# A fused attention and mixture-of-experts kernel: gathers set ahead of scatter-adds one tile behind, the shared weights fetched behind the last context rows, the first scores ahead of the second bias fold

## The chip, the cores and the metric

One Trainium2 chip, one of its cores. The metric is the device time of one execution in microseconds, the median of several runs. Before the change: 547.0 us, three runs from 546.81 to 549.09.

## The reference

`x` is 16 sequences of 56 rows of 512; each has a context of 1500 rows of 512. In float32:

```python
xn = layernorm(x)
Q  = xn @ Wq + bq;  K = ctx @ Wk + bk
x  = x + softmax(Q @ K.T / sqrt(512)) @ ctx         # 16 sequences, 56 x 1500 scores each
hn = layernorm(x)                                   # 896 rows
s  = sigmoid(hn @ gate.T) + bias                    # 16 experts
w, idx = top_k(s, 4);  w = w / (sum(w) + 1e-20)     # 4 experts of each row
out = sum over picked experts e of  w_e * (silu(hn @ Wg_e.T) * (hn @ Wu_e.T)) @ Wd_e.T
out = out + (silu(hn @ Sg.T) * (hn @ Su.T)) @ Sd.T  # a shared expert, for all rows
x   = x + out
```

The experts' inner width is 256. Which rows go to which expert is known only when the gate has run.

## The kernel before

**Attention.** The two projections are folded into one matrix, Wq Wk^T (`fold`), and two bias terms: a column for the queries' side (`fold_cols`) and a row (`fold_c`, `c_row`). Sequences go in 8 pairs, two side by side in the 128 lanes. A pair's context comes twice: transposed in four blocks (`ctx_cols`, 1.5 MB each) for the scores and as rows in three groups (`ctx_rows`, 2 MB each) for the weighted sum. There is one set of each, so SP reloads a block as soon as TensorE has used it (`cols_used`, `rows_used`). SP's queue works its transfers off in order; behind the first pair's rows it issues the shared expert's weights (`shared_raw`) and a block of zero rows, and only then the second pair's blocks. While a pair is scored, the gate and the rank of each row in its experts' lists are worked out for the pair before it.

**Shared stage.** 7 tiles of 128 rows go through the shared expert (t = 0 to 6). ScalarE casts its weights to a high part and VectorE takes the rest to a low part, so that each product is three fast matmuls (hi*hi, hi*lo, lo*hi). Meanwhile VectorE makes the plan: tables of 48 entries, one entry for each expert tile (which list column, which expert, which weights to split before it, how many turns). `lay_tables` puts them into one row, and each engine reads its entries by `value_load` (an instruction TENSOR_LOAD on its queue). The lists of rows (`list_at` to gather from, `list_to` to add to) have one column for each expert and tile.

**Expert stage.** 34 tiles of gathered rows here (t = 7 to 40), in the order of the experts, 11 turns of weights. Two buffers of each kind; tile t uses buffer t % 2. TensorE's order in one step t is: transpose z(t-1), the low part of up(t), transpose the gathered tile t+1, down(t-1), the high part of up(t+1). ScalarE in its step t: zt_hi(t-1), tanh(t), taken_hi(t+1), `keep_y(t-2)` (copies down's result to `y_sb`, once the scatter-add that read this buffer has landed), `name_add(t-2)` (copies the row numbers of that add), and the casts of weights that the plan asks for. VectorE: zt_lo(t-1), silu(t), taken_lo(t+1), the weight of each row of tile t+1, `name_take(t+3)` (the row numbers of a gather), and the low parts of the weights.

POOL issues all gathers and scatter-adds, in order, and waits in between:

```python
add(t, 1 - k)          # waits: adds of earlier experts landed, add_named, ysb_ready of t
gather(t + 5, k)       # waits: take_named of t + 5
```

An add reads and writes rows of `out` in HBM. Adds of one expert never meet in a row; an add waits until all adds of earlier experts have landed. SP loads a turn's weights (`w_raw`, 1.5 MB) when the low parts of two turns before are done, and waits for their landing.

## Time and profile before

| | |
|---|---|
| median of 3 runs | 547.0 us |
| the profiled execution | 546.24 us |
| its span | 544.5 us |
| mean granted TensorE clock | 0.96 |
| one turn of the attention loop on TensorE | 29.43 us (scores start at 66.11, 95.54, 124.97) |
| last third of attend, first shared matmul | 274.02 to 277.6, 277.61 us |
| gathered tile 13's taken_hi | 364.05 us |
| ScalarE casts of expert weights, L897 | 33, mean 1047 ns |
| VectorE low parts of them, L1280 | 33, mean 1223 ns |
| last scatter-add issued | 532.9 us |

Times of an execution are a little more than its span, which runs from the first to the last instruction of the trace. All start times in the text count from the span's start. Lines (L459) are lines of the kernel before. TensorE's clock has two levels here, 1.2 and 2.4 GHz; the granted clock is a share of 2.4. `L680` is the helper of all expert matmuls, `L500` all transposes of four blocks. A gather is `taken<-h_rows,take_at`, a scatter-add `out<-y_sb,add_at`.

### The profile page before, as it was taken

What the parts mean: (1) busy time and instruction counts of PE and PEld (TensorE: products, weight loads), DVE (VectorE), ACT (ScalarE), POOL (GpSimd) and SP (SyncE); (2) the same over time, 40 slices, a digit from 0 to 9 for tenths busy, and PEclk for the clock granted to TensorE, in tenths of its full rate; (3) what the DMA queues carried; (4) which work ended last, traced back from release to release, by engine and by line L of the source; (5) the groups of instructions that cost most, each with busy time, mean ns of one, the idle gap of its engine ahead of it and who ended that gap; (6) DMA issues with size and microseconds to landing.
All of it is one profiled execution on the core that took longest, in us unless ns stands there. A gap on an engine that the chain in (4) does not pass through costs nothing.

```text
span 544.5 us, 10804 instructions
## 1 busy us (share of the span) xinstructions
PE 481.4 (88%) x2472; PEld 291.5 (54%) x2473; DVE 260.0 (48%) x707; ACT 155.8 (29%) x303; POOL 119.3 (22%) x100
## 2 busy tenths in 40 slices
PE   4999999999999999998789869779998898899960
PEld 1565354453636363543358636567776666676740
DVE  3223345462737354352537864625565466555420
ACT  0001321020202020210213253435455456444430
POOL 1000000000000000000002233335554465335531
PEclk9989999999999999999899979979999899899985
DMA  9999999999999999999646676785858687445452
GB/s 212 393 419 427 398 424 415 409 427 396 424 402 426 403 422 404 422 426 415 258 127 174 150 202 191 235 254 94 221 100 265 137 207 210 78 88 98 98 64 32
DMA packets 28231, 149.04 MB, mean 274 GB/s; under 512 B 4072, under 2 KB 4200, under 8 KB 16424
## 3 DMA queue, kind: packets, MB, share of 16 engines
q1 hardware_dynamic: 15832, 123.08, 57.1%
q0 software_dynamic: 8720, 20.21, 20.5%
q10 hardware_dynamic: 3664, 5.57, 3.3%
q8 instruction: 7, 0.11, 0.1%
q14 instruction: 8, 0.07, 0.0%
HBM read 133.84 MB, written 15.01 MB: 273 GB/s over the span
## 4 chain that ended last, share of the span: by engine, by line
PE 49%; DMA 33%; issue 7%; DVE 3%; ACT 2%; POOLq 1%; ACTq 1%; POOL 1%; DVEq 1%; SPq 0%
DMA ctx_cols<-in_ctx_t 15%; PE b L680 13%; PE scores L550 11%; PE b L574 8%; DMA taken<-h_rows,take_at 8%; DMA out<-y_sb,add_at 5%; PE b L538 4%; PE b L500 4%; PE scores L512 2%; PE scores L680 2%; PE b L564 1%; DMA w_qk<-in_wk 1%; DMA out<-y_sb,shared_at 1%; DMA h_rows<-h 1%; POOL out L459 1%
## 5 line engine op out<-in xcount | busy, mean ns | idle before, releaser
L550 PE MATMUL scores<-ctx_cols,g_t 128*64 128x500 f32 x384 | 85.2, 586 | 2.6 <-DMA ctx_cols<-in_ctx_t 2.5
L574 PE MATMUL b<-ctx_rows,probs_t 125*64 125x512 f32 (+1 forms) x384 | 86.0, 598 | 0.0
L459 POOL DMA_INDIRECT out<-y_sb,add_at x34 | 54.5, 1604 | 89.0 <-ACT add_at L931 46.8
L423 POOL TENSOR_TENSOR rstd<-var_eps,neg_half 128x1 f32<-128x1 f32 x16 | 8.8, 549 | 268.4 <-DVE var_eps L1022 268.4
L680 PE MATMUL b<-w_hi,taken_hi 128*128 x136 | 56.2, 414 | 1.1 <-ACT taken_hi L908 1.1
L680 PE MATMUL b<-w_lo,taken_hi 128*128 x136 | 54.8, 403 | 0.0
L1280 DVE TENSOR_TENSOR w_lo<-w_raw,w_hi (+1 forms) x33 | 39.7, 1223 | 30.2 <-ACT w_hi L897 26.6
L550 PEld LDWEIGHTS scores<-ctx_cols,g_t 128*64 128x64 f32 x384 | 26.1, 136 | 51.8 <-issue 46.0
L574 PEld LDWEIGHTS b<-ctx_rows,probs_t 125*64 125x64 f32 (+1 forms) x384 | 26.3, 137 | 48.0 <-issue 47.1
L444 POOL DMA_INDIRECT taken<-h_rows,take_at x34 | 42.7, 1257 | 28.4 <-DVE take_at L1306 20.2
L897 ACT CAST w_hi<-w_raw (+1 forms) x33 | 33.8, 1047 | 29.0 <-PE b L680 9.1
L500 PE MATMUL b<-cst,taken 128*128 128x128 f32 x164 | 26.6, 287 | 17.1 <-DMA taken<-h_rows,take_at 15.2
L680 PE MATMUL b<-w_hi,taken_lo 128*128 x136 | 40.0, 416 | 0.0
L1053 DVE TENSOR_REDUCE row_max<-scores 128x1 f32<-128x1500 f32 x8 | 13.8, 1721 | 50.4 <-PE scores L550 50.4
L836 ACT COPY h_t_now<-b 128x512 f32<-128x512 f32 x7 | 4.1, 585 | 110.6 <-PE b L500 110.6
L500 PEld LDWEIGHTS b<-cst,taken 128*128 128x128 f32 x164 | 19.5, 146 | 28.3 <-issue 25.8
L1299 DVE TENSOR_TENSOR taken_lo<-b,taken_hi 128x512 fp32r<-128x512 f32 x41 | 28.1, 685 | 11.6 <-ACT taken_hi L908 11.6
L538 PE MATMUL b<-xn_t,w_fold 128*128 128x128 f32 x256 | 32.0, 286 | 1.4 <-ACT xn_t L820 1.4
L680 PEld LDWEIGHTS b<-w_hi,taken_hi 128*128 128x128 f32 x136 | 26.8, 197 | 11.0 <-issue 4.9
L908 ACT CAST taken_hi<-b 128x512 fp32r<-128x512 f32 x41 | 24.0, 587 | 30.1 <-PE b L500 28.6
L538 PEld LDWEIGHTS b<-xn_t,w_fold 128*128 128x128 f32 x256 | 30.7, 200 | 1.9 <-issue 1.0
L918 ACT CAST zt_hi<-b 128x256 fp32r<-128x256 f32 x41 | 15.2, 371 | 54.4 <-PE b L703 54.1
(213 smaller groups left out, 677.2 us busy)
## 6 DMA issues: line engine op xcount, KB each, us to landing
ctx_rows<-in_ctx SPq DMA_DIRECT2D x48, 1024.0 KB, 19.5
ctx_cols<-in_ctx_t SPq DMA_DIRECT2D x32, 1500.0 KB, 22.8
w_raw<-in_experts SPq DMA_DIRECT2D x11, 1536.0 KB, 7.5
h_rows<-h ACTq DMA_DIRECT2D x16, 115.5 KB
taken<-h_rows SPq DMA_DIRECT2D x7, 264.0 KB, 3.1
out<-xs ACTq DMA_DIRECT2D x2, 784.0 KB
shared_raw<-in_shared SPq DMA_DIRECT2D x1, 1536.0 KB, 32.4
xs<-in_x ACTq DMA_DIRECT2D x12, 112.0 KB
```

Of the source, the lines that this page charges most:

```text
L444: nc.gpsimd.indirect_dma_start(taken[i][:, :], None, h_rows[:, :], bass.IndirectOffsetOnAxis(ap=take_at[i][:, 0:1], axis=0)).then_inc(gath ...
L459: nc.gpsimd.indirect_dma_start(out[:, :], bass.IndirectOffsetOnAxis(ap=add_at[i][:, 0:1], axis=0), y_sb[:, i * DIM:(i + 1) * DIM], None, c ...
L500: last = nc.tensor.transpose(bank[:, k * P:(k + 1) * P], src[:, k * P:(k + 1) * P], ident)
L538: last = nc.tensor.matmul(b7[:, m * P:(m + 1) * P], w_fold[:, k, m * P:(m + 1) * P], xn_t[:, k, :], start=(k == 0), stop=(k == KD - 1))
L550: last = nc.tensor.matmul(scores[HALF * b:HALF * (b + 1), n, 0:CHUNK], g_t[:, k, HALF * b:HALF * (b + 1)], ctx_cols[:, at:at + CHUNK], sta ...
L574: last = nc.tensor.matmul(b3[HALF * b:HALF * (b + 1), :], probs_t[0:rows_in(p), at:at + HALF], ctx_rows[0:rows_in(p), g, b, c * DIM:(c + 1 ...
L680: return nc.tensor.matmul(bank, a[:, k, :], w[:, bass.ds(at + k * n, n)], start=start, stop=stop)
L897: nc.scalar.copy(w_hi[:, bass.ds(at, THIRD)], w_raw[:, bass.ds(at, THIRD)]).then_inc(hi_ready, 1)
L908: nc.scalar.copy(taken_hi[:].rearrange("p k n -> p (k n)"), b4[:, :]).then_inc(taken_hi_ready, 1)
L918: nc.scalar.copy(zt_hi_cols[:], b5[:, 0:INNER]).then_inc(zt_hi_ready, 1)
L1280: nc.vector.tensor_tensor(w_lo[:, bass.ds(at, THIRD)], w_raw[:, bass.ds(at, THIRD)], w_hi[:, bass.ds(at, THIRD)], ALU.subtract).then_inc(l ...
L1299: nc.vector.tensor_tensor(taken_lo[:].rearrange("p k n -> p (k n)"), b4[:, :], taken_hi[:].rearrange("p k n -> p (k n)"), ALU.subtract).th ...
```

## The change

1. SP issues `shared_raw` and the zero rows behind the last pair's context rows. ScalarE's three casts and VectorE's three low parts move from behind the first pair to behind the last pair's probabilities.
2. The query bias column is no longer made by 40 narrow matmuls, but by four wide ones into b4, whose diagonal blocks VectorE sums out. The scalar bq*bk comes from VectorE and one matmul. The first two score blocks stand ahead of `fold_c`.
3. The row numbers of the tiles are picked once: the list of places is transposed on TensorE (`lay_places`), kept by ScalarE and multiplied by a 0/1 matrix (`pick_tiles`), so that tile t has its own column in `tile_at` and `tile_to`. Reads of the plan for them fall away on VectorE and ScalarE.
4. A gather is issued ahead of the scatter-add, for the tile six ahead, and waits for the transposes of the tile that had its buffer. The add's row numbers are copied by POOL. On VectorE the weight and the name of the next gather stand ahead of silu.
5. SP issues the loads of the first two turns' weights one behind the other.

```diff
@@ SP
-            sp.dma_start(shared_raw[:], shared).then_inc(shared_loaded, 16)
-            sp.wait_ge(init_ready, 1)
-            sp.dma_start(h_rows[TOKENS:TOKENS + P, :], zero_rows[:]).then_inc(init_stored, 16)
...
             reload_cols(PAIRS - 2)
             reload_rows(PAIRS - 2)
+            sp.dma_start(shared_raw[:], shared).then_inc(shared_loaded, 16)
+            sp.wait_ge(init_ready, 1)
+            sp.dma_start(h_rows[TOKENS:TOKENS + P, :], zero_rows[:]).then_inc(init_stored, 16)
...
             load_raw(0)
             load_raw(1)
+            sp.wait_ge(raw_first, 16)
+            sp.sem_inc(raw_ready, THIRDS)
+            raw_there(1)
@@ POOL
             def gather(t, i):
                 pool.wait_ge(take_named, t - (SHARED - 1))
                 settle(pool)
+                pool.wait_ge(tt_ready, t - 1)
+                settle(pool)
...
             def add(t, i):
                 first = entry(pool, T_FIRST, t - SHARED, TILES + SHARED)
-                pool.wait_ge(added[0], pool.snap((first + 1) // 2 * 16 + 16, min_val=16, max_val=16 * TILES))
+                pool.wait_ge(added[i], t // 2 * 16 + 16)
                 settle(pool)
-                pool.wait_ge(added[1], pool.snap(first // 2 * 16 + 16, min_val=16, max_val=16 * TILES))
-                settle(pool)
-                pool.wait_ge(add_named, t - (SHARED - 2))
+                nc.gpsimd.tensor_copy(add_at[i][:], tile_to[:, bass.ds(t - SHARED, 1)]).then_inc(add_named, 1)
+                others = first // 2 if i == 0 else (first + 1) // 2
+                pool.wait_ge(added[1 - i], pool.snap(others * 16 + 16, min_val=16, max_val=16 * TILES))
                 settle(pool)
                 pool.wait_ge(ysb_ready, t + 1)
+                settle(pool)
+                pool.wait_ge(add_named, t + 1)
...
-            add_shared(3)
             pool.wait_ge(init_stored, 16)
             pool.wait_ge(h_stored, PAIRS * 32 + 16)
...
             gather(SHARED, 1)
             gather(SHARED + 1, 0)
+            add_shared(3)
             add_shared(4)
             gather(SHARED + 2, 1)
             gather(SHARED + 3, 0)
             add_shared(5)
             gather(SHARED + 4, 1)
             add_shared(6)
+            gather(SHARED + 5, 0)
...
                     t = pair * 2 + (SHARED + k)
+                    gather(t + 6, 1 - k)
                     add(t, 1 - k)
-                    gather(t + 5, k)
@@ TensorE
-                for m in range(KD):
-                    for k in range(KD):
-                        last = nc.tensor.matmul(b7[:, m:m + 1], wk_sb[:, k, m * P:(m + 1) * P], bq_sb[:, k:k + 1],
-                                                start=(k == 0), stop=(k == KD - 1))
                 for k in range(KD):
-                    last = nc.tensor.matmul(b7[:, KD:KD + 1], bq_sb[:, k:k + 1].to_broadcast([P, P]),
-                                            bk_sb[:, k:k + 1], start=(k == 0), stop=(k == KD - 1))
+                    last = nc.tensor.matmul(b4[:, :], bq_sb[:, k:k + 1].to_broadcast([P, P]), wk_sb[:, k, :],
+                                            start=(k == 0), stop=(k == KD - 1))
...
+            def lay_places():
+                pe.wait_ge(plan_ready, 1)
+                pe.wait_ge(places_ready, 1)
+                nc.tensor.transpose(scores[:, 2, 0:P], place_at[:], ident).then_inc(places_laid, 1)
+            def pick_tiles():
+                pe.wait_ge(places_kept, 1)
+                nc.tensor.matmul(scores[:, 2, P:P + AHEAD], place_t[:], tile_picks[:], start=True, stop=True
+                                 ).then_inc(tiles_picked, 1)
...
             project(0)
+            score(0, 0)
+            score(0, 1)
             fold_c()
-            for k in range(KD):
-                score(0, k)
+            score(0, 2)
+            score(0, 3)
...
             shared_transpose(6)
+            lay_places()
             down(4, 0, shared_hi, shared_lo, 0)
+            pick_tiles()
@@ ScalarE
-            act.wait_ge(shared_loaded, 16)
-            act.wait_ge(fold_ready, KD + 2)
-            for n in range(THIRDS):
-                nc.scalar.copy(shared_hi[:, n * THIRD:(n + 1) * THIRD], shared_raw[:, n * THIRD:(n + 1) * THIRD]
-                               ).then_inc(shared_hi_ready, 1)
...
             store_h(last_pair - 1)
+            act.wait_ge(shared_loaded, 16)
+            act.wait_ge(fold_ready, KD + 3)
+            for n in range(THIRDS):
+                nc.scalar.copy(shared_hi[:, n * THIRD:(n + 1) * THIRD], shared_raw[:, n * THIRD:(n + 1) * THIRD]
+                               ).then_inc(shared_hi_ready, 1)
...
                 keep_y(t - 2, i)
-                if not isinstance(t, int):
-                    name_add(t - 2, i)
                 more_thirds(t + 1)
@@ VectorE
             def name_take(t, i):
-                col = entry(dve, T_COL, t - SHARED, LISTS + EXPERTS - 1)
-                nc.vector.tensor_copy(take_at[i][:], list_at[:, bass.ds(col, 1)]).then_inc(take_named, 1)
+                nc.vector.tensor_copy(take_at[i][:], tile_at[:, bass.ds(t - SHARED, 1)]).then_inc(take_named, 1)
             def take_weight(t, i):
-                e = entry(dve, T_EXPERT, t - SHARED, EXPERTS - 1)
-                nc.vector.tensor_copy(taken_w[:, i:i + 1], taken[i][:, bass.ds(e + DIM, 1)]).then_inc(w_ready, 1)
+                dve.wait_ge(gathered[i], (t - SHARED) // 2 * 16 + 16)
...
+                nc.vector.scalar_tensor_tensor(picked_w[:, i * EXPERTS:(i + 1) * EXPERTS], iota16, expert_row[:, bass.ds(t - SHARED, 1)],
+                                               taken[i][:, DIM:ROW], ALU.is_equal, ALU.mult, accum_out=taken_w[:, i:i + 1]
+                                               ).then_inc(w_ready, 1)
...
             def step(t, i):
                 z_to_lo(t - 1)
+                take_weight(t + 1, 1 - i)
+                name_take(t + 3, 1 - i)
                 silu_rows(t, i)
                 taken_to_lo(t + 1)
-                take_weight(t + 1, 1 - i)
-                name_take(t + 3, 1 - i)
                 more_thirds(t + 1)
```

One step of POOL's loop in the expert stage, before (L459 is the add, L444 the gather, 1024x512 the whole of `out`):

```order
L323 TENSOR_LOAD plan
L323 ISA x2
L451 ISA
L453 ISA
L455 REGISTER_ALU
L457 REGISTER_ALU
L459 DMA out<-y_sb,add_at 1024x512
L442 REGISTER_ALU
L444 DMA taken<-h_rows,take_at 128x528
```

and after (L469 is the gather, L486 the add):

```order
L467 REGISTER_ALU
L469 DMA taken<-h_rows,take_at 128x528
L335 ISA
L335 TENSOR_LOAD plan
L335 ISA x2
L476 ISA
L478 ISA
L478 COPY add_at<-tile_to 128x1
L480 ISA
L482 REGISTER_ALU
L486 DMA out<-y_sb,add_at 1024x512
```

The gather now stands first, and between it and the add there is one more operation of POOL itself.

SP's queue at its start, before, with the shared weights behind the first pair's blocks and ahead of the loop of reloads:

```order
L305 DMA xs<-in_x 56x512 x4
L342 DMA ctx_cols<-in_ctx_t 128x3000 x4
L348 DMA ctx_rows<-in_ctx 128x2048 x6
L357 DMA shared_raw<-in_shared 128x3072
L359 DMA h_rows<-zero_rows 128x528
L371 UNCONDITIONAL_BRANCH
```

and after, behind that loop, where the last pair's blocks are issued:

```order
L355 DMA ctx_cols<-in_ctx_t 128x3000 x4
L361 DMA ctx_rows<-in_ctx 128x2048 x6
L386 DMA shared_raw<-in_shared 128x3072
L388 DMA h_rows<-zero_rows 128x528
L411 DMA taken<-h_rows 128x528 x7
```

Both transfers moved from the head of the queue to just ahead of the shared tiles' loads (L411).

## Rows read from the trace of the kernel before

**Rows 1.** The page: busy time of TensorE; the chain that ended last, by engine.
```profile
PE 481.4 (88%) x2472; PEld 291.5 (54%) x2473; DVE 260.0 (48%) x707; ACT 155.8 (29%) x303; POOL 119.3 (22%) x100
...
PE 49%; DMA 33%; issue 7%; DVE 3%; ACT 2%; POOLq 1%; ACTq 1%; POOL 1%; DVEq 1%; SPq 0%
```
**Rows 2.** Windows: stretch, length, busy (count) by engine, clock, DMA share, GB/s.
```profile
30.00:31.00 1.00, 1.00 (x5) 1.00 (x6) 0.00 (x0) 0.00 (x0) 0.00 (x0) 0.50 1.02 430
...
120.00:240.00 120.00, 117.32 (x700) 55.52 (x697) 59.12 (x176) 18.47 (x32) 4.38 (x8) 1.00 1.01 414
...
268.00:270.00 2.00, 2.00 (x12) 0.64 (x10) 0.00 (x0) 0.00 (x0) 0.00 (x0) 1.00 0.12 48
```
**Rows 3.** The chain in order of time, attention: start us, us, what.
```profile
24.23 3.46 PE b L519 x32
...
29.85 5.30 PE b L538 x32
35.15 3.44 PE b L529 x8
...
50.06 3.84 PE b L538 x32
...
66.11 5.03 PE scores L550 x24
...
254.05 2.76 PE scores L550 x12
```
**Rows 4.** Timeline, expert stage, TensorE and VectorE: start us, us, operation [idle before].
```profile
379.31 0.48 PE L680 MATMUL b<-w_hi,zt_hi 128*128 x1
...
389.15 0.42 DVE L1315 TENSOR_TENSOR zt_lo<-b,zt_hi 128x256 fp32r<-128x256 f32 x1 [1.45 <-ACT zt_hi L918]
...
389.64 0.48 PE L680 MATMUL b<-w_hi,zt_hi 128*128 x1
```
**Rows 5.** Timeline of ScalarE: first and last taken_hi of the 34 gathered tiles.
```profile
322.19 0.59 ACT L908 CAST taken_hi<-b 128x512 fp32r<-128x512 f32 x1 [3.80 <-PE b L500]
...
518.04 0.59 ACT L908 CAST taken_hi<-b 128x512 fp32r<-128x512 f32 x1
```
**Rows 6.** Waits of the whole span: us, times, longest.
```profile
PE b L500 <- DMA taken<-h_rows,take_at: 15.2, 9, 5.2
...
ACT y_sb L926 <- DMA out<-y_sb,add_at: 5.4, 2, 4.6
```
**Rows 7.** The chain, expert stage.
```profile
348.47 8.02 DMA taken<-h_rows,take_at
```
**Rows 8.** Timeline of the first 62 us, SP and VectorE.
```profile
18.61 3.13 SPq L357 DMA_DIRECT2D shared_raw<-in_shared  x1
...
57.36 3.50 DVE L1198 TENSOR_TENSOR shared_lo<-shared_raw,shared_hi 128x1024 fp32r<-128x1024 f32 x3 [2.67 <-ACT shared_hi L878]
```
**Rows 9.** DMA issues from 48.5 to 50 us: KB, us to landing.
```profile
ctx_cols<-in_ctx_t SPq DMA_DIRECT2D x1, 1500.0 KB, 18.5
```
**Rows 10.** Timeline around the first gather.
```profile
313.13 0.16 DVE L1306 COPY take_at<-list_at 128x1 int32 x1 [1.16 <-issue]
...
314.18 1.02 POOL L444 DMA_INDIRECT taken<-h_rows,take_at  x1 [0.97 <-DVE take_at L1306]
```
**Rows 11.** Timeline, expert stage: POOL, ScalarE and TensorE.
```profile
387.27 1.57 POOL L459 DMA_INDIRECT out<-y_sb,add_at  x1 [1.56 <-DMA out<-y_sb,add_at]
392.15 1.05 ACT L897 CAST w_hi<-w_raw  x1 [0.95 <-PE b L680]
396.08 0.59 ACT L926 COPY y_sb<-b 128x512 f32<-128x512 f32 x1
493.67 1.57 POOL L459 DMA_INDIRECT out<-y_sb,add_at  x1 [0.39 <-issue]
526.54 0.49 PE L680 MATMUL b<-w_hi,zt_hi 128*128 x1 [1.96 <-ACT zt_hi L918]
```
**Rows 12.** The 34 scatter-adds (L459), from POOL's issue to landing.
```profile
DMA to landing us min/median/max: 4.5/4.9/8.8
```

More of the change, by code:

```diff
@@ L484, in _ @@
                     t = pair * 2 + (SHARED + k)
+                    gather(t + 6, 1 - k)
                     add(t, 1 - k)
-                    gather(t + 5, k)
             t = n_inner * 2 + (SHARED - 2)
-            add(t, 1)
-            gather(t + 5, 0)
-            for k in range(1, 6):
+            for k in range(6):
                 add(t + k, 1 - k % 2)
@@ L613, in lay_tables @@
                 last.then_inc(table_rows_ready, 1)
+                for at, column in ((C_PICK, place_col), (C_EXPERT, expert_t)):
+                    last = nc.tensor.matmul(scores[:, 0, at:at + AHEAD], column[:].to_broadcast([P, P]),
+                                            ident[:, 0:AHEAD], start=True, stop=True)
+                last.then_inc(picks_ready, 1)
+            def lay_places():
[6 more added lines that the diff above has]
+                                 ).then_inc(tiles_picked, 1)
             pe.sem_inc(ht_ready, 1)
@@ L1154, in _ @@
             nc.vector.tensor_copy(shared_at[:], shared_place[:]).then_inc(shared_named, 1)
[L1155 to L1157 removed]
+            ch.mark(nc.vector.tensor_scalar(place_at[:, LISTS:], dump_row[:].to_broadcast([P, EXPERTS]), -float(P), None,
+                                            ALU.add))
             wide = [P, PAIRS, TILES_MAX]
```

149 lines of the change are left out of this document (91 added, 58 removed).

## The prediction

> **What bounds the kernel now.** I read the busy table and the chain that ended last first, then windows of the attention stage, then the engines' rows in the expert stage. TensorE is busy for 88% of the span, but the chain is only half TensorE: a third of it is transfers [rows 1], column blocks in the first half, gathers and scatter-adds in the second.
>
> In the attention stage (to 265 us) the 16 DMA engines never rest: 414 GB/s at a share of 1.01, with TensorE at 117.3 of 120 us [rows 2]. One turn of the loop costs TensorE 29.43 us (the table above), and its 12.44 MB at 414 GB/s cost the queue 30.0 us. So the queue falls 0.6 us a turn behind, and the last turns wait for column blocks, as at 254.05 [rows 3]. Both limits are close: without waits the last score, 11.0 us behind its turn's start, would have ended at 66.11 + 6*29.43 + 11.0 = 253.7; it ended at 256.8. The first of the two moves with TensorE's start, the second with bytes.
>
> In the expert stage (34 gathered tiles) the tile's work on TensorE is 5.15 us: down matmuls start at 379.31 and 389.64, two tiles apart [rows 4]. From the first to the last tile 195.85 us pass (322.19 to 518.04) [rows 5] for 33 intervals, 5.93 each: 26 us are waits. The wait table gives TensorE 15.2 us, nine times, for gathers [rows 6]; the longest, 5.2 us, ends with a gather of 8.02 us that POOL issued at 348.47 behind a scatter-add [rows 7]. The rest is weights: casts by threes and late loads.
>
> **Front and attention.** (1) The shared weights and the zero rows, 1.57 + 0.27 MB, leave their place ahead of the second pair [rows 8]: 1.84 MB / 414 GB/s = 4.4 us earlier for everything behind. The queue does not run dry for it: the last column block of a pair, issued near 49.0, lands 18.5 us later, at 67.5 [rows 9], while the next row blocks are issued at 59.4; 4.4 less leaves 3.7 us of queued work, and each turn adds its 0.6. (2) Fold: 32 + 8 narrow matmuls, 3.46 us and by the same rate 0.9, become 4 wide ones like the 3.44 us of L529 [rows 3]: -0.9. The first projection took 5.30 us, the next 3.84, and at 30 to 31 us the granted clock was 0.50, the lower level, after TensorE had stood idle for most of the microsecond before it [rows 2, 3]. Whether wide matmuls ahead of it keep the clock up no row shows: 0 to 1.5 us; I take half, 0.7. Scores begun before fold_c leave open the g_t wait that fold_c covered (g_t took 0.69, some 0.95 with latencies): +0.95. VectorE's four diagonal sums lie beside the transpose and the projection. TensorE's limit: 253.7 - 0.9 - 0.7 + 0.95 = 253.0. The queue's limit: 254.05 - 4.4 + 2.76 = 252.4. I take 253.1, a gain of 3.7.
>
> (3) The shared weights now come last. All bytes until then are the same, so the engines still fall quiet near 267.7 (48 GB/s at 268 to 270) [rows 2]; by then shared_raw is there. Casts: VectorE's three subtractions took 3.50 us [rows 8] and began some 1.2 behind the first cast's start (a cast is 1.05): 267.8 to 272.5. TensorE meanwhile transposes the first shared tile and does the last third of attend (3.6 us from 274.02 before), which it now does near 270.4 to 274.0. So the casts are covered by 1.5 us; if the load lands 3 us later, they are the new wait and cost 1.5. The stage starts 3.5 us earlier: **-3.5**.
>
> (4) The first gather gets a longer way: the list goes through a transpose on TensorE, a ScalarE copy and one more matmul. Before, the name was written at 313.13 and the gather began at 314.18 [rows 10]. Now, on the same clock, the list's float places are there near 311.0 (two VectorE steps less than before, which ended near 312), TensorE waits for them ahead of down(4), which had begun at 309.95, so +1.2; ScalarE copies near 312, TensorE picks behind down(4) at 313.2, the name follows at 313.8: the gather 0.6 later, bounded by 0 and 3 (the longest wait is TensorE's for the list). I take **+0.6**. The second expert's weights no longer wait until the first has landed; it takes at most the 1.15 us that tile 8 lost, and I count nothing.
>
> **The expert loop, gathers.** A gather is now issued as soon as its buffer is free. 15.2 us of waits [rows 6], less the first, 3.1 us, which is the way above, plus about 1.5 us of matmuls at the lower clock behind the 5.2 us wait, is 13.6 us: **-13.6**, all of it if nothing else comes late. 6.8 of it lies before tile 13.
>
> **The expert loop, scatter-adds.** What is late next is the y_sb buffer. POOL is in order, and add(t) now stands behind gather(t+6), which needs the transposes of tile t+4; before, it only needed y(t), there about when tile t+3 is transposed. Example from the rows: add(14) began at 387.27, and y(16), the same buffer, was copied at 396.08 [rows 11]. The add landed before it, with 4 us to spare at the usual 4.9 us [rows 12]; ScalarE waited for an add only twice, 5.4 us [rows 6], at the very end. Now: down(16) on TensorE begins at 389.64, zt_lo ends 389.57 [rows 4]; taking the weight and the name add some 0.5: 390.05; name to gather 0.89 (313.13 + 0.16 to 314.18) [rows 10]: 390.9; gather 1.0, gap 0.39 as at 493.67 [rows 11]: 392.3; the new POOL copy of add_at, which no row shows: 0.1 (a memset) to 0.55 (POOL's small rstd operation), with its own semaphore I take 0.6: 392.9. It lands 4.9 later, 397.8, **1.7 us after y(16) was wanted**.
>
> What that does to TensorE: y(16) at 397.9; the weight cast follows 1.14 us behind the last small operation's start (0.19 of it and the 0.95 idle at 392.15) and takes 1.05: 400.1; zt_hi(18) 0.37: 400.55; TensorE 0.53 later, as at 526.54 behind a zt_hi that ended at 526.01 [rows 11]: 401.1. From down(16) to down(18) that is **11.45 us for two tiles in place of 10.3**. ScalarE spares 0.6 by no longer copying add_at, which is in this sum. Where VectorE's w_lo (1.22 us in the table) stands ahead of the zt_lo that starts the chain, it is 12.4. Without a cast in the step 10.3 to 11.1. Casts fall in 18 of the 27 steps behind tile 13 (ScalarE's timeline; 33 thirds are cast in all), so by their shares 0.45*12.4 + 0.22*11.4 + 0.22*11.1 + 0.11*10.3 = 11.66 for two, 5.83 a tile, 157.4 us for 27 tiles where 139 would be free of waits. Adds that meet a weight load landed after 6.7 to 8.8 us, five of them behind tile 13, 2.6 over the usual on the average; the spare time that hid this is gone: 13, of which I take 9, since some fall on other waits. 4 us of weight waits stay. Together 170 against the 154.0 that these 27 intervals took: **+16.4**, in which the gather gain of this stretch is already counted. Tiles 7 to 13: 41.9 before (322.19 to 364.05, the table), less 6.8, plus 2 for the first late y: **-4.9**. Tail: adds 35 and 36 have to catch up; between 0 and 3 (adds of different experts follow each other by their landing and about 1 us, against a tile's 5.15) I take **+0.5**.
>
> The Trainium skill bears on this in "DMA: Bandwidth & Descriptors", "Anatomy of one DMA": for a POOL-issued transfer 2.0 us plus bytes over 436 GB/s. By that an add of 256 KB would take 2.6 us and land at 395.5, ahead of y(16): no new wait, the faster rival below. The trace disagrees, with 4.5 us as the least of 34 adds [rows 12]. "SBUF — State Buffer", "SBUF: two separate sides", says that VectorE operations of some kinds and GpSimd lock each other out of a shared port for a whole instruction; by that the new POOL copy could wait behind a VectorE operation and come later still, up to the 1.23 us of w_lo. No row of before shows that copy; the sum goes by 0.6.
>
> **Sum.** -3.5 + 0.6 - 4.9 + 16.4 + 0.5 = +9.1. The profiled execution took 546.24 us (span 544.5 and 1.7 around it); 546.24 + 9.1 = 555.3. The median of the runs is 0.8 above it: **556**.
>
> **Rivals.** *A, the adds stay hidden (faster).* If the add starts sooner behind the gather or ScalarE has more room than I give it, only the gather gain is left: -13.6 - 3.5 + 0.6 = -16.5, about 530 with the 0.8. For it: the wait is only 1.7 us in the example, and it must come on most tiles. The point from which it decides: an add that lands within 7.3 us of the transposes it waits for (I have 8.1). Against it: 4 us of spare time are used up by 5.7 us of delay. Chance 0.27, time 525 to 543. *B, a draw.* Late y copies cost what the gathers give (about 14 + 3), as when only the adds beside weight loads come late: 544.3 to 549.7, at 547. Chance 0.11. *C, the shared casts on the path.* The attention gain shrinks to nothing (3.5) and the rest stays: 559.5; it lies inside the forecast's range.
>
> **How the numbers follow.** Forecast, slower: 0.62, own range 550 to 567 (every step with a cast at 12.4 and all congested adds late: +11; adds 0.6 us sooner and the rest half hidden: -6). A measurement of this kernel tells 0.5%, 2.7 us, from no change: faster 0.27 (A), same 0.11 (B), slower 0.62. The range from 531 to 569 leaves out the lower half of A (0.1) and some 0.07 above.
>
> **What would show it.** Attention: scores of the last pair end near 253, the first shared matmul starts near 274. Expert stage: hardly any TensorE wait for gathers; in its place a long row "ScalarE y_sb waits for DMA out" (some 1.7 us, over 20 times) and TensorE waiting for zt_hi or zt_lo; adds starting some 3.2 us behind the transposes of tile t+4; tile spacing near 5.8 to 6.1. The prediction is wrong if y_sb hardly waits for adds, or if it waits and TensorE still runs at 5.2 to 5.4 a tile, or if the shared weights land after 271.

## The result, and the profile after

The changed kernel took **565.49 us** (median of 4 runs, 565.09 to 568.1); the kernel before, on the same chip, 546.9 (4 runs, 543.52 to 549.09). The ratio is 1.036, 95% interval 1.029 to 1.042. The profiled execution took 565.76 us, with a span of 563.7; against the span before, 544.5, that is +19.2 where the sum had +9.1. The direction and the mechanism were those of the prediction, the size was not. Every ratio here leaves out the runs that another state of the chip had lengthened; the medians keep them.

The page: TensorE's busy time and the chain that ended last, by engine and by line. The chain's share of DMA was 33% before [rows 1].

```profile
PE 490.0 (87%) x2445; PEld 292.4 (52%) x2446; DVE 260.5 (46%) x753; ACT 148.8 (26%) x269; POOL 120.8 (21%) x134
...
PE 54%; DMA 18%; issue 12%; ACT 4%; DVE 3%; ACTq 2%; POOLq 1%; DVEq 1%; POOL 1%; SPq 0%
PE scores L576 15%; DMA out<-y_sb,add_at 14%; PE b L600 14%; PE b L724 8%; PE b L564 5%; PE b L527 2%; PE scores L539 2%; PE b L590 2%; ACT w_hi L944 2%; DMA h_rows<-h 1%; DMA w_qk<-in_wk 1%; ACTq L335 1%; DMA w_raw<-in_experts 1%; PE scores L724 1%; PE b L613 1%
```

Of the DMA share 14 points are now one kind of transfer, the scatter-adds. The waits of the whole span (us, times, longest) say who stands for them:

```profile
ACT y_sb L973 <- DMA out<-y_sb,add_at: 76.2, 27, 5.9
POOL taken L469 <- issue: 73.5, 26, 6.8
DVE w_lo L1331 <- ACT w_hi L944: 67.5, 21, 7.2
...
DVE zt_lo L1369 <- ACT zt_hi L965: 40.7, 19, 5.4
...
ACT zt_hi L965 <- PE b L747: 39.7, 18, 5.0
...
PE b L527 <- DMA taken<-h_rows,take_at: 2.6, 2, 1.8
```

TensorE's waits for gathers went from 15.2 us to 2.6; ScalarE's wait for an add, ahead of the y_sb copy, went from 5.4 us to 76.2 [rows 6]. Below it stand those who come behind ScalarE: VectorE waits 67.5 us for casts and 40.7 for zt_hi, where it waited 26.6 and 26.2 before.

By stages, from ScalarE's timeline (first, seventh and last taken_hi of the gathered tiles; they answer to 322.19, 364.05 and 518.04 [rows 5] and the table there):

```profile
321.03 0.58 ACT L955 CAST taken_hi<-b 128x512 fp32r<-128x512 f32 x1 [2.12 <-issue]
...
357.47 0.59 ACT L955 CAST taken_hi<-b 128x512 fp32r<-128x512 f32 x1
...
537.96 0.59 ACT L955 CAST taken_hi<-b 128x512 fp32r<-128x512 f32 x1
```

| stretch | before | after | change | forecast |
|---|---|---|---|---|
| start to tile 7 (attention, shared stage, first gather) | 322.19 | 321.03 | -1.2 | -2.9 |
| tiles 7 to 13 | 41.86 | 36.44 | -5.4 | -4.9 |
| 27 intervals behind tile 13 | 153.99 | 180.49 | **+26.5** | **+16.4** |
| tile 40 to the end | 26.46 | 25.74 | -0.7 | +0.5 |
| span | 544.5 | 563.7 | +19.2 | +9.1 |

All of the miss, 10.1 us, is in the third line.

A "cycle" below is the way from an operation to the same one two tiles later, when the same buffer comes round again. One such cycle of the third line, from the timeline near the end, where no weights load beside it:

```profile
515.10 0.42 DVE L1369 TENSOR_TENSOR zt_lo<-b,zt_hi 128x256 fp32r<-128x256 f32 x1
515.58 0.15 DVE L1355 COPY take_at<-tile_at 128x1 int32 x1
516.74 0.98 POOL L469 DMA_INDIRECT taken<-h_rows,take_at  x1 [2.73 <-issue]
517.72 0.20 POOL L478 COPY add_at<-tile_to 128x1 int32 x1
518.77 1.61 POOL L486 DMA_INDIRECT out<-y_sb,add_at  x1 [0.85 <-ACT y_sb L973]
523.64 0.59 ACT L973 COPY y_sb<-b 128x512 f32<-128x512 f32 x1 [2.58 <-DMA out<-y_sb,add_at]
524.79 1.05 ACT L944 CAST w_hi<-w_raw  x1 [0.57 <-issue]
525.74 0.37 ACT L965 CAST zt_hi<-b 128x256 fp32r<-128x256 f32 x1
526.17 1.23 DVE L1331 TENSOR_TENSOR w_lo<-w_raw,w_hi  x1 [4.19 <-ACT w_hi L944]
526.64 0.49 PE L724 MATMUL b<-w_hi,zt_hi 128*128 x1 [1.17 <-ACT zt_hi L965]
527.32 0.42 DVE L1369 TENSOR_TENSOR zt_lo<-b,zt_hi 128x256 fp32r<-128x256 f32 x1
527.80 0.15 DVE L1355 COPY take_at<-tile_at 128x1 int32 x1
```

Name 515.58, gather 1.16 later, add 2.03 behind the gather, the copy of y into the same buffer 4.87 behind the add, the cast, zt_hi, VectorE's w_lo ahead of zt_lo, the next name: 12.22 us for two tiles. It is the chain of the prediction, link by link, with its "12.4 where w_lo stands ahead"; what is missing is in the cycles that are not like this one.

In the third line TensorE's granted clock was 0.92 in the mean, 0.98 before, and its busy time 154.9 us for 142.6. That slower matmuls set the length is not what the runs show: in e4 below the same stretch takes the same 180.4 us with a clock of 0.94 and 151.8 us busy.

### The profile page after: what moved, and what is told of

It reads as the page before. It is cut to its first block, busy times and chain, and to the rows that moved or that the text cites. A ratio compares the mean times of both kernels' runs of the same rounds, so it can differ in the third digit from the quotient of the medians.

```text
span 563.7 us, 10463 instructions
## 1 busy us (share of the span) xinstructions
PE 490.0 (87%) x2445; PEld 292.4 (52%) x2446; DVE 260.5 (46%) x753; ACT 148.8 (26%) x269; POOL 120.8 (21%) x134
## 4 chain that ended last, share of the span: by engine, by line
PE 54%; DMA 18%; issue 12%; ACT 4%; DVE 3%; ACTq 2%; POOLq 1%; DVEq 1%; POOL 1%; SPq 0%
PE scores L576 15%; DMA out<-y_sb,add_at 14%; PE b L600 14%; PE b L724 8%; PE b L564 5%; PE b L527 2%; PE scores L539 2%; PE b L590 2%; ACT w_hi L944 2%; DMA h_rows<-h 1%; DMA w_qk<-in_wk 1%; ACTq L335 1%; DMA w_raw<-in_experts 1%; PE scores L724 1%; PE b L613 1%
## 5 line engine op out<-in xcount | busy, mean ns | idle before, releaser
L600 PE MATMUL b<-ctx_rows,probs_t 125*64 125x512 f32 (+1 forms) x384 | 87.5, 606 | 0.0
L1331 DVE TENSOR_TENSOR w_lo<-w_raw,w_hi (+1 forms) x33 | 39.8, 1225 | 73.6 <-ACT w_hi L944 67.5
L486 POOL DMA_INDIRECT out<-y_sb,add_at x34 | 55.6, 1634 | 37.6 <-ACT y_sb L973 17.4
L724 PE MATMUL b<-w_hi,taken_hi 128*128 x136 | 59.3, 436 | 1.2 <-ACT taken_hi L955 1.1
L724 PE MATMUL b<-w_lo,taken_hi 128*128 x136 | 57.5, 423 | 0.0
L469 POOL DMA_INDIRECT taken<-h_rows,take_at x34 | 34.4, 1012 | 98.6 <-issue 73.5
L1369 DVE TENSOR_TENSOR zt_lo<-b,zt_hi 128x256 fp32r<-128x256 f32 x41 | 17.3, 422 | 41.0 <-ACT zt_hi L965 40.7
L724 PEld LDWEIGHTS b<-w_hi,taken_hi 128*128 128x128 f32 x136 | 28.6, 210 | 13.2 <-issue 6.5
L724 PE MATMUL b<-w_hi,zt_hi 128*128 x34 | 15.2, 448 | 19.2 <-ACT zt_hi L965 18.7
L564 PE MATMUL b<-xn_t,w_fold 128*128 128x128 f32 x256 | 30.6, 278 | 1.4 <-ACT xn_t L867 1.4
L724 PEld LDWEIGHTS b<-w_lo,taken_hi 128*128 128x128 f32 x136 | 28.4, 209 | 6.1
L564 PEld LDWEIGHTS b<-xn_t,w_fold 128*128 128x128 f32 x256 | 29.2, 192 | 1.9 <-issue 1.0
```

Of the source, the lines that this page charges most:

```text
L469: nc.gpsimd.indirect_dma_start(taken[i][:, :], None, h_rows[:, :], bass.IndirectOffsetOnAxis(ap=take_at[i][:, 0:1], axis=0)).then_inc(gath ...
L486: nc.gpsimd.indirect_dma_start(out[:, :], bass.IndirectOffsetOnAxis(ap=add_at[i][:, 0:1], axis=0), y_sb[:, i * DIM:(i + 1) * DIM], None, c ...
L564: last = nc.tensor.matmul(b7[:, m * P:(m + 1) * P], w_fold[:, k, m * P:(m + 1) * P], xn_t[:, k, :], start=(k == 0), stop=(k == KD - 1))
L600: last = nc.tensor.matmul(b3[HALF * b:HALF * (b + 1), :], probs_t[0:rows_in(p), at:at + HALF], ctx_rows[0:rows_in(p), g, b, c * DIM:(c + 1 ...
L724: return nc.tensor.matmul(bank, a[:, k, :], w[:, bass.ds(at + k * n, n)], start=start, stop=stop)
L1331: nc.vector.tensor_tensor(w_lo[:, bass.ds(at, THIRD)], w_raw[:, bass.ds(at, THIRD)], w_hi[:, bass.ds(at, THIRD)], ALU.subtract).then_inc(l ...
```

## The experiments

Times are medians; "before" was run on the same chip each time (543.0 in the first four, 543.6 in the next four, 548.0 in the three after them, 554.1 in the last, where the ratio is to runs from 542.8 to 550.2), so kernels of different groups are compared by their ratios, and by the stages of their traces. The last column is the stretch from tile 13 to tile 40 in the profiled execution.

| kernel | us | ratio to before (95%) | 27 intervals |
|---|---|---|---|
| changed | 565.5 | 1.036 (1.029 to 1.042) | 180.5 |
| e1 add first | 537.8 | not given; all runs (530.2 to 539.2) below all of before (541.3 to 548.3) | 152.3 |
| e2 before, gather first | 601.4 | 1.100 (1.092 to 1.108) | 220.4 |
| e3 four y_sb buffers | 533.6 | 0.980 (0.975 to 0.986) | 150.2 |
| e4 shared weights early | 565.8 | 1.041 (1.034 to 1.047) | 180.4 |
| e5 name late | 588.1 | 1.081 (1.075 to 1.087) | 198.5 |
| e6 = e3, attend first | 534.8 | 0.983 (0.978 to 0.988) | 148.9 |
| e7 = e3, add first | 547.2 | 1.006 (1.002 to 1.010) | 163.8 |
| e8 = e3, loads one by one | 537.8 | 0.989 (0.983 to 0.994) | 149.9 |
| e9 copy ahead of gather | 564.7 | 1.028 (1.019 to 1.037) | 178.4 |
| e10 = e6, copy ahead | 534.6 | 0.976 (0.970 to 0.983) | 150.3 |
| e11 = e1, attend first | 534.0 | 0.977 (0.970 to 0.983) | 151.9 |
| e12 casts ahead of y_sb copy | 556.9 | 1.018 (1.007 to 1.030) | 172.4 |

**e1, POOL's old order in the changed kernel.**

```diff
-            gather(SHARED + 5, 0)
...
-                    gather(t + 6, 1 - k)
                     add(t, 1 - k)
+                    gather(t + 5, k)
```

> The changed kernel with POOL's loop in the old order: add(t), then the gather of tile t+5; all else of the change stays. Theory Y (the loss is ScalarE's y_sb copy waiting for scatter-adds that are issued a tile later): the 76.2 us of y_sb waits shrink to under 8, TensorE's waits for gathers return, and the time falls from 565.5 to 540 to 548. Theory W (the loss comes from the rest of the new expert path: VectorE's weight and name ahead of silu, POOL's own copy, two weight loads at once): the order alone gives back little, 558 or more.

Measured 537.8, a little below the 540 to 548 expected: the order alone costs 28 us, all of it in the 27 intervals (152.3 for 180.5), and the rest of the change is a gain. On this chip e4, which is the changed kernel in all that bears on the loop, took 565.8. The waits:

```profile
PE b L528 <- DMA taken<-h_rows,take_at: 8.5, 6, 4.7
...
ACT y_sb L974 <- DMA out<-y_sb,add_at: 6.4, 2, 5.0
```

**e2, the new order in the kernel before.** `gather(t + 6, 1 - k)` ahead of `add(t, 1 - k)`, nothing else.

> The kernel before with one edit: POOL issues gather(t+6) ahead of add(t), so the add stands a tile behind; row numbers, VectorE and ScalarE as before. Theory Y: ScalarE's y_sb waits appear here too (over 50 us) and the time rises from 547 to 560 to 568. Theory W: 543 to 550, with fewer waits for gathers.

Measured 601.4: the direction as expected, the size far outside. In place of 5.7 us a tile it took 8.2 (in a profiled execution of 611.75 us, 1.7% above that median, so its figures are somewhat high). The timeline shows why; the name of a gather and what stands ahead of it in one step:

```profile
524.37 0.37 ACT L917 CAST zt_hi<-b 128x256 fp32r<-128x256 f32 x1 [0.70 <-issue]
...
524.90 0.42 DVE L1314 TENSOR_TENSOR zt_lo<-b,zt_hi 128x256 fp32r<-128x256 f32 x1 [2.15 <-issue]
...
525.24 0.41 DVE L1335 SCALAR_TENSOR_TENSOR gated_rows<-half_tanh,b 128x256 f32<-128x256 f32 x1
...
525.80 0.48 DVE L1323 SCALAR_TENSOR_TENSOR z_rows<-gated_rows,taken_w,b 128x256 f32<-128x256 f32 x1
526.20 0.68 DVE L1298 TENSOR_TENSOR taken_lo<-b,taken_hi 128x512 fp32r<-128x512 f32 x1
526.85 0.15 DVE L1309 COPY taken_w<-taken 128x1 f32 x1
527.68 0.15 DVE L1305 COPY take_at<-list_at 128x1 int32 x1 [0.68 <-issue]
528.68 0.98 POOL L444 DMA_INDIRECT taken<-h_rows,take_at  x1 [1.46 <-DVE take_at L1305]
```

Here the name comes 3.3 us behind zt_hi (524.37 to 527.68), in the changed kernel 1.2 (518.85 to 520.05): silu, taken_lo and a read of the plan stand ahead of it. POOL stands for names through the whole loop:

```profile
POOL taken L444 <- DVE take_at L1305: 137.7, 34, 11.8
```

With the gather in front of the add the name is a link of the cycle. The expectation had left it out.

**e3, four y_sb buffers in the changed kernel.** `y_sb` is 4 x 512 wide, tile t uses part t % 4, the copy waits for the add of four tiles ago, and POOL picks one of two fixed adds by a branch:

```diff
-                act.wait_ge(added[i], t // 2 * 16 + 16)
+                act.wait_ge(added[i], t // 2 * 16)
...
+                for half in range(2):
+                    pool.reg_mov(slot, pool.snap((t // 2 + half) % 2, min_val=0, max_val=1))
+                    with pool.If_lt(slot, 1):
+                        at = (2 * half + i) * DIM
```

> The changed kernel with four y_sb buffers in place of two (a copy waits for the add four tiles back; POOL picks the buffer by two short branches). Gathers stay ahead, adds stay a tile behind. Theory Y: y_sb waits all but vanish, nothing is late for gathers either, tile spacing falls from 6.57 to about 5.3 and the time to 525 to 535. Theory W: 555 or more.

Measured 533.6, in theory Y's range, 32 us below the changed kernel with the same order on POOL; a tile takes 5.6 us where 5.3 was expected. No y_sb wait for an add is left among the waits. It is the prediction's rival A once y_sb no longer holds the copies back: its time was 525 to 543.

**e7, four buffers and the add first** (e3 with e1's order), which completes the table of order by buffers.

> The four-buffer kernel with POOL's old order (the add first, the gather five ahead behind it). It tells what the gather-first order is worth once y_sb has four buffers. Theory Y as in the prediction's faster rival: gather waits cost the add-first order its 8.5 us of TensorE waits and DVE's 6.5, so gather-first gains 4 to 8 us: this one 537 to 541 against 533.6. Rival D: the two orders are equal once nobody waits for y_sb, since a gather's wait only moves to another place (the weight casts): 532 to 535.

Measured 547.2, 13.6 us above e3 and above even e1, which lies outside both expectations. Its waits:

```profile
POOL out L495 <- issue: 83.6, 31, 5.4
...
PE b L538 <- DMA taken<-h_rows,take_at: 19.9, 10, 4.9
```

TensorE waits 19.9 us for gathers where e1 has 8.5. Adds now start later, 2.4 us behind their y copy in the mean of tiles 12 to 37 against 1.8 in e1, and each gather behind an add with them. That the branch on POOL, which comes with the four buffers, is what makes the adds later is likely but not shown by itself. So: two buffers 537.8 (add first) and 565.5 (gather first); four buffers 547.2 and 533.6. Neither order is good by itself; gather first pays only if y_sb does not wait. Of its 13.6 us with four buffers a part may be the branch's cost in e7: against e1, which has neither branch nor turned order, e3 gains 4 us, and as e1's runs lie between 530.2 and 539.2, even that is not certain.

**e5, only VectorE's name and weight put back behind silu and taken_lo.**

```diff
                 z_to_lo(t - 1)
-                take_weight(t + 1, 1 - i)
-                name_take(t + 3, 1 - i)
                 silu_rows(t, i)
                 taken_to_lo(t + 1)
+                take_weight(t + 1, 1 - i)
+                name_take(t + 3, 1 - i)
```

> The changed kernel with one thing put back: VectorE takes the weight and the name of the next gather behind silu and taken_lo again, instead of ahead of silu. Theory N: with the gather ahead of the add, the name is a link of the chain name, gather, add, landing, y_sb copy, next name. In the kernel before with only POOL's order turned, a cycle of two tiles took 16.5 us, 3.3 more than the 13.2 of the changed kernel, all of it between the y_sb copy and the next name. So 13.5 cycles by 3.3 = 44 us more than the changed kernel: 600 to 612. Rival R: the slowness of that kernel came from its other old parts (the plan reads on VectorE and ScalarE, the add's numbers copied by ScalarE); then 565 to 575 here.

Measured 588.1, between the two: the 27 intervals take 18.0 us more than in the changed kernel, of the 39.9 that e2's trace takes more. So the name's place is a link, and worth 1.3 us a cycle, not 3.3. The rest of e2 lies in its other old parts and, in part, in the length of its profiled execution: the 0.68 us read of the plan ahead of the name is in the rows above, the others were not taken apart.

**e9, POOL's copy of the row numbers ahead of the gather.**

```diff
+                    name_add(t, 1 - k)      # waits for added[i], copies add_at
                     gather(t + 6, 1 - k)
                     add(t, 1 - k)
```

> The changed kernel with one thing moved: POOL copies the add's row numbers ahead of the gather instead of between gather and add. It measures the slope of the chain (name, gather, add, landing, y_sb copy, next name). Theory Y: in the changed kernel 2.03 us pass from the gather's start to the add's, 0.98 of them the gather, 0.20 the copy and 0.85 between the copy and the add. Without the copy there some 0.3 to 0.4 remain behind the gather, so a two-tile cycle is 0.65 to 0.75 us shorter by the gap and copy together less what stays, and at most 1.05: 13.5 cycles make 9 to 14 us less than the changed kernel, 551 to 557. Rival G: the 0.85 us belong to the reads of the plan's entry and the registers between gather and add, not to the copy; then only the copy's own 0.2 goes, 2.7 us: 561 to 564.

Measured 564.7, above both ranges, 551 to 557 and 561 to 564; with runs from 559.6 to 567.5 and a ratio whose interval overlaps that of the changed kernel, no difference can be told. POOL's rows here, to set beside 516.74, 517.72 and 518.77 above:

```profile
517.36 1.00 POOL L469 DMA_INDIRECT taken<-h_rows,take_at  x1 [1.54 <-issue]
519.00 1.59 POOL L488 DMA_INDIRECT out<-y_sb,add_at  x1 [0.64 <-ACT y_sb L977]
```

Gather to add fell by 0.39 us (2.03 to 1.64), less than the 0.65 expected, since 0.64 stays behind the gather without any copy. In the quiet cycles at the end that arrives in full: 12.19 to 12.22 us became 11.75. Over all 27 intervals only 2.1 of 13.5 by 0.39 = 5.3 us arrived, and the stretches before and behind gave it back. The edit also brought something of its own. The copy waits for the add two tiles back to land, and now does so ahead of the gather (5.6 us, six times). And it now falls beside VectorE's w_lo:

```profile
514.06 1.76 POOL L476 COPY add_at<-tile_to 128x1 int32 x1
514.57 1.23 DVE L1335 TENSOR_TENSOR w_lo<-w_raw,w_hi  x1 [4.06 <-ACT w_hi L948]
```

The same copy that took 0.2 us in the changed kernel takes 1.76 here and ends 0.02 us behind w_lo; 11 of the 34 do the like, with 0.8 to 1.8 us. The gather was not held up by it (it starts 1.2 us behind its name, as in the changed kernel), but e9 is no clean measure of the slope. The fixed part of the way from name to add was, by its own rows, not what the forecast had missed: 2.03 us against 2.0.

**e12, ScalarE's casts ahead of the y_sb copy.** Counting the casts between taken_hi rows of the changed kernel, a pair of tiles with none takes 11.9 us (2 pairs), with one 12.9 (11 pairs, 12.2 where nothing else is late), with two 13.6 (8 pairs). The means lie closer together than the pairs of one group do (11.4 to 16.1 with one cast), so the count alone shows little, and the cast was moved.

```diff
                 taken_to_hi(t + 1)
-                keep_y(t - 2, i)
                 more_thirds(t + 1)
+                keep_y(t - 2, i)
```

> The changed kernel with two calls of ScalarE's step swapped: the casts of weights stand ahead of the y_sb copy instead of behind it. In the changed kernel a pair of tiles with no cast takes 11.9 us (mean of 2), with one 12.9 (12.2 where nothing else is late), with two 13.6, with three and more 14.4: the copy waits for the add's landing and every cast stands behind it, ahead of zt_hi. Theory K: the casts are a link of the cycle, and the forecast was short because it counted one at most for two tiles. Ahead of the copy they lie in the 2.8 us in which ScalarE waits for the landing anyway, so the 27 intervals behind tile 13 fall from 180.5 towards 27/2 by 11.9 = 161 and the whole to 546 to 554. Rival: the cast has to wait for down(t-1), some 2.4 us behind the transposes, and pushes the copy back by as much as it gives: 560 to 568, with y_sb's wait for the add shorter and nothing gained.

Measured 556.9, between the two again (the intervals of its ratio and of the changed kernel's just touch): the 27 intervals fall by 8.1 us, tiles 7 to 13 by 1.1. VectorE's wait for casts falls to 37.1 from 67.5. Two pieces of the timeline of this kernel show both halves of it, the cast in the wait, and the cast that holds the copy back:

```profile
444.45 1.05 ACT L944 CAST w_hi<-w_raw  x1 [1.16 <-PE b L724]
451.22 0.58 ACT L973 COPY y_sb<-scores 128x512 f32<-128x512 f32 x1 [5.72 <-DMA out<-y_sb,add_at]
...
456.26 1.61 POOL L486 DMA_INDIRECT out<-y_sb,add_at  x1 [0.86 <-POOL add_at L478]
461.41 1.05 ACT L944 CAST w_hi<-w_raw  x1 [1.16 <-PE b L724]
462.37 0.58 ACT L973 COPY y_sb<-scores 128x512 f32<-128x512 f32 x1
```

In the first the cast lies ahead of a 5.7 us wait and costs nothing. In the second the add of 456.26 lands 4.9 us later, at 461.2, but ScalarE, which stood 1.2 us for TensorE's down, has only just begun the cast, and the copy comes 1.2 us late, at 462.4. Over the stretch the way from the copy to the next zt_hi fell from 2.7 to 0.8 us a cycle, while the way from an add to the copy that waits for it rose from 5.4 to 6.5 and that from gather to add from 2.2 to 2.9. So moving the casts is shown to be worth 8 us in all; what they would be worth without this payment, and how far the rest of the 10 goes with them, stays open.

**e4, the shared weights back at the front of the queue**, with their casts.

```diff
@@ SP, behind the first pair's blocks
+            sp.dma_start(shared_raw[:], shared).then_inc(shared_loaded, 16)
...
@@ SP, behind the last pair's rows
-            sp.dma_start(shared_raw[:], shared).then_inc(shared_loaded, 16)
```

> The changed kernel with the shared weights' load and casts back behind the first pair. Theory S (the late load bought 4 us of scores and lost them to the row store, 7.4 us in place of 5.5, and to the lower clock behind TensorE's longer stand): scores end 3 us later again, the first shared matmul starts where it did, 276.5 to 278, and the time stays within 2 us of 565.5. Theory C (the shared casts themselves are on the path): the first shared matmul comes 3 us earlier and the time falls to 562.

Measured 565.8, as expected: fetching the shared weights late is worth nothing here. The chain of the changed kernel, in order of time (start, us, what), shows what ate the 4 us that the scores had gained:

```profile
252.64 1.73 DVE row_max L1095
...
261.40 7.44 DMA h_rows<-h
268.86 2.76 DMA taken<-h_rows
...
271.76 0.99 PE b L527 x4
272.75 4.86 PE b L600 x16
277.61 2.52 PE b L724 x10
```

The scores end at 252.6, as forecast (near 253), 4.2 us earlier than before. Then the store of the last rows takes 7.44 us, 1.9 more than before; TensorE stands for 3 us, and its transposes and the last third of attend take 1.6 us more (4.86 us the latter, 3.58 before); 0.6 is lost between scores and store. Why the store took longer is not shown. Windows (length, busy by engine, clock, DMA share, GB/s), first the changed kernel, then e4:

```profile
272.00:276.00 4.00, 4.00 (x14) 1.41 (x14) 3.50 (x6) 1.32 (x2) 0.00 (x0) 0.59 0.24 68
```

```profile
272.00:276.00 4.00, 3.45 (x32) 1.66 (x32) 1.15 (x3) 0.59 (x1) 0.00 (x0) 1.00 0.54 176
```

Behind the stand the granted clock is 0.59 in the mean, part of it at the lower level; in e4, with 0.55 us of waiting, it is 1.00. In both the first shared matmul starts at the same time, 277.5, though e4's scores end 4.5 us later.

**e6 and e11, TensorE's last third of attend ahead of the first shared transposes**, in e3 and in e1:

```diff
-            shared_transpose(0)
             attend(last_pair, 2)
+            shared_transpose(0)
```

> The four-buffer kernel with TensorE's order at the end of attention turned: the last third of attend ahead of the first shared tile's transposes. Theory S: the late shared load freed TensorE 4 us earlier, and it lost that standing for the row load (3.6 us idle, then 4.7 us of attend at the lower clock instead of 3.6). With attend in that gap the first shared matmul begins at 274.4 to 274.8 (bounded by shared_lo, done near 274.4) instead of 277.8, and the whole is 3.0 to 3.4 us shorter than the four-buffer kernel: 529.5 to 531. Rival C: something else holds the shared stage (the shared weights' low parts, or the last pair's own chain through the gate to the lists): first matmul earlier, but the first gather still near 315.0, and the whole within 1 us of 533.6.

> The changed kernel with POOL's old order (add first) and TensorE's last third of attend ahead of the first shared transposes. There no y_sb wait and no chain of adds sets the end, so the 2.6 us by which the shared stage begins earlier can be seen. Theory S: the late shared load's gain had been lost to TensorE's standing and lower clock at 268 to 277, and comes back: 1.2 (what reached tile 7 in the four-buffer kernel) to 2.6 us below the 537.8 of the add-first kernel: 535.2 to 536.6. Rival C: the first gathered tiles wait for the first expert's weights, and it is lost there: 537 to 539.

TensorE in e6:

```profile
269.95 3.65 PE L610 MATMUL b<-ctx_rows,probs_t 125*64 125x512 f32 x16
...
273.53 0.66 PE L537 MATMUL b<-cst,taken 128*128 128x128 f32 x4
...
275.16 0.47 PE L734 MATMUL b<-shared_hi,taken_hi 128*128 128x512 f32 x1 [0.97 <-ACT taken_hi L965]
```

Attend takes 3.65 us again and the first shared matmul starts at 275.16 instead of 277.80. The first gather starts 2.55 us earlier (312.47 for 315.02). Yet e6 took 534.8 against e3's 533.6: nothing gained, outside theory S's 529.5 to 531, while the first gather moved, which rival C had ruled out. POOL's last add in e3 and in e6:

```profile
520.53 1.57 POOL L495 DMA_INDIRECT out<-y_sb,add_at  x1 [1.17 <-issue]
```

```profile
520.44 1.57 POOL L495 DMA_INDIRECT out<-y_sb,add_at  x1 [1.17 <-issue]
```

TensorE is 1.5 us ahead at tile 40 and the last add is not: with four buffers the adds run behind and set the end. In e11 nothing of the kind does. Its tile 7 comes 2.8 us before that of e1 (318.25 for 321.07) and its span is 3.5 shorter (531.4 for 534.9); by the medians it is 534.0, below the 535.2 to 536.6 expected, but on another chip, and the runs of the two overlap (532.7 to 540.7 and 530.2 to 539.2). By the traces theory S holds: the attention gain had been lost on TensorE's standing and lower clock. It was not tried in the changed kernel itself.

**e10, e6 with POOL's copy ahead of the gather.**

> The four-buffer kernel with attend ahead of the first transposes, and POOL's copy of the row numbers ahead of the gather. In that kernel TensorE ended 1.5 us earlier than in the plain four-buffer kernel and the last add still began at 520.4. Theory E: the adds set the end there, so a shorter way to each add gives 1 to 2.5 us: 532 to 534 against 534.8. Rival: the end hangs on the landing of each add before the next (the last six adds are 3 to 6 us apart with the copy already in their shadow), and nothing moves: 534 to 536.

Measured 534.6, so the rival: no difference from e6 beyond what the runs can tell (the intervals of the two ratios overlap). The tail from tile 40 on is 31.1 us there, 29.2 in e6, 27.9 in e3: what comes sooner on TensorE waits longer at the end.

**e8, the second expert's weights fetched only when the first have landed**, in e3.

```diff
             load_raw(0)
-            load_raw(1)
             sp.wait_ge(raw_first, 16)
             sp.sem_inc(raw_ready, THIRDS)
+            load_raw(1)
```

> The four-buffer kernel with the second expert's weights loaded only when the first have landed, as before the change. The prediction counted nothing for this edit, 1.15 us at most. Theory: ScalarE's cast of the second turn starts 0.5 to 1.5 us later and tile 8 with it: the whole 0 to 1.2 us longer than the four-buffer kernel, 533.6 to 534.8. Rival: the startup gain of 5.4 us (tiles 7 to 13) came from it: 536 to 539, with the interval from tile 7 to 13 back at 37 to 40 us from 33.7.

Measured 537.8, 4.2 us above e3 (on another chip; the intervals of the ratios overlap a little): more than the 1.2 allowed, and in the rival's 536 to 539. In the traces tile 7 comes 1.7 us later and the way from 7 to 13 is 36.5 us, against 33.7. The prediction had counted this edit as nothing; it is worth about 4 us where the adds leave it visible.

## Why the prediction came out as it did

**Right.** That y_sb's wait for the add takes the place of TensorE's wait for gathers, and that it costs more: e1 and e3 take the two halves of it away, one by order, one by buffers, and each returns 28 to 32 us. The sequence of links, and 12.4 us for a cycle with a cast (12.2 measured). The scores' end at 253, the first gather 0.6 later than before at an unchanged start of the shared stage (314.76 for 314.18).

**Right in part by luck: tiles 7 to 13, -5.4 for -4.9.** The term was made of gather waits (-6.8) and a late y (+2), and counted the two weight loads issued one behind the other as nothing. In e8 these are worth 2.8 us of just this stretch. In the changed kernel they were not tried alone; if they are worth as much there, the rest of the term brought about 2.6 us and not 4.9.

**Wrong, the size: the loop's cycle, "by their shares ... = 11.66 for two, 5.83 a tile, 157.4 us for 27 tiles ... Together 170".** With the 9 us for late adds and the 4 for weights that is 12.6 us for two tiles; it was 13.37, 180.5. The third line's 25 cycles that can be followed whole, from the y copy of tiles 10 to 34 to the copy two tiles on, give the links in the mean. The forecast's column is worked out from the times and shares in its own example:

| link, start to start | forecast | measured |
|---|---|---|
| y copy, (casts), zt_hi, (w_lo), zt_lo | 2.9 | 3.9 |
| zt_lo to the name | 0.7 | 0.6 |
| name to gather | 1.0 | 1.2 |
| gather to add | 2.0 | 2.2 |
| add to the y copy that waited for it | 5.0 + 0.7 for late adds | 5.4 |
| weight waits | 0.3 | |
| sum | 12.6 | 13.3 |

The step that failed is the first link, priced by shares of steps with a cast and without: it is 1.0 us a cycle longer, 13 us in 13.5 cycles, more than all of the miss; the late adds came out a little cheaper than feared. The forecast had zt_hi start 2.2 us behind the copy with a cast between and 1.1 without. It counted a step with three casts as one, and such cycles (3 of the 25) take 4.0 us. And it had zt_hi start as soon as ScalarE was free, but in 8 of the 25 zt_hi waited 0.8 to 3.7 us for TensorE's transposes of z (L747): cycles without a cast took 2.2 to zt_hi, those with one 2.7. e12 moved the casts out of the link and got 8.1 us back, net of what it cost elsewhere, so that part is shown. No experiment parts the wait for TensorE from the rest; whether it too comes from the casts, those of the tile beside, stays open. The other links are not it: POOL's copy was sized 0.6 with its semaphore, gather to add 2.0, and 2.03 was measured where nothing else waits; making that 0.39 shorter changed nothing that the medians show (e9).

**Wrong, but small: the attention gain of 3.5 us was zero.** The step was "TensorE meanwhile transposes the first shared tile and does the last third of attend (3.6 us ...), which it now does near 270.4 to 274.0". It looked at casts and at bytes, and not at the row store in front of the transposes, 7.44 us now for 5.5 us before, nor at the clock behind TensorE's standing. The casts, rival C, were not on the path: shared_lo was done at 274.4, attend at 277.6. The start of tile 7 was still 1.2 us earlier. The two loads one behind the other, which the forecast called nothing, bring tile 7 forward by 1.7 us in e8, which may be where that came from.

**Rival A** (adds stay hidden, 525 to 543, chance 0.27) is what e3 measured, with the one cause removed that the forecast had named for it not to come true.

Of the prediction's two sentences on the Trainium skill the trace decides both. By "DMA: Bandwidth & Descriptors" ("Anatomy of one DMA") of the Trainium skill an add of this size would take 2.6 us, an estimate from its figures, and the wait would have stayed hidden; the trace speaks against it, as y_sb is free only 4.87 us behind the add's start in the cycle above. "SBUF — State Buffer" ("SBUF: two separate sides") of the Trainium skill has VectorE and GpSimd lock each other out for a whole instruction in certain pairs. In the changed kernel no POOL copy ran beside a w_lo, and 31 of 34 took 0.18 to 0.21 us; in e9, where copies did, they ended with w_lo after up to 1.76 us, and there the trace agrees.

## What to carry to other kernels

Before an in-order queue is turned so that one kind of transfer goes first, write down the cycle that closes behind it, from the name of one transfer to the release of the buffer and back, and put into it every operation that stands between on every engine, with the number of them that each turn has and the waits for other engines, not only this engine's own work. A double buffer whose release has moved past another wait needs more depth or the old order: here the gathers' new place cost 28 us with two buffers, and with four buffers they gained 14 against the old order, though perhaps only 4 against the old order with two buffers. And work that ends earlier gains nothing if the next step waits for a store to land: 4.2 us of scores were lost in that gap, and 2.6 came back at the first shared matmul when the last third of attend, which needs no store, was put into it.

## What the runs showed of the hardware

- A POOL copy of 128 numbers takes 0.20 us, but the next indirect DMA starts 0.85 us behind it; without the copy 0.64 us behind the gather (e9), and a gather 0.30 behind an add where it waits for nothing (e1, e7).
- The last third of attend, 16 matmuls, took 3.65 us right behind other work and 4.86 to 4.93 behind 3 us of standing, at a granted clock of 0.59 in the mean; behind 0.55 us of standing (e4) they took 3.65 at 1.00.
- A POOL copy that ran beside VectorE's w_lo, whose two inputs both lie in SBUF, ended 0.02 to 0.04 us behind it: 0.8 to 1.8 us for 11 copies of e9, against 0.18 to 0.21 for 31 of 34 in the changed kernel.
- From POOL's issue of a scatter-add of 256 KB to the y copy that waited for it 5.4 us passed in the mean of 25 in the changed kernel, 4.7 us at the least.
